# Interleaving the value projections with the chunk preparation, splitting the first inversion between GpSimd and VectorE, and starting the chunk loop one late-layer step later

## The reference

```python
q = _causal_conv_silu(x @ Wq.T, conv_q)     # also k, and v (128 wide a head)
q, k = _l2_norm(q), _l2_norm(k)
alpha = jnp.exp(-jnp.exp(A_log) * jax.nn.softplus(a_lin + dt_bias))
beta = 2.0 * jax.nn.sigmoid(x @ Wb.T)
...
S = a_t * (S - b_t * kkS) + jnp.einsum('bhd,bhv->bhdv', k_t, v_t)
o_t = jnp.einsum('bhdv,bhd->bhv', S, q_t)
```

## Time and profile before

| quantity | value |
|---|---|
| median of three runs | 9192.65 us |
| the profiled execution | 9168.5 us, span 9166.7 us |
| mean granted TensorE clock | 0.884 of full speed |
| TensorE matmul busy | 7076.2 us, 77% |
| VectorE busy | 4884.4 us, 53% |
| GpSimd busy | 2815.9 us, 31% |
| ScalarE busy | 2654.0 us, 29% |
| bytes moved by DMA | 225.76 MB, 25 GB/s |

### The profile page before, as it was taken

How to read it: one execution, slowest core, us unless ns; L and a number is a source line. 1 busy time by engine, 2 the same in 40 slices (tenths; PEclk the granted TensorE clock), 3 DMA queues, 4 the chain that set the end, 5 groups by cost and what they waited for, 6 DMA issues and landing times. The chain is left out here.

```text
span 9166.7 us, 157275 instructions
## 1 busy us (share of the span) xinstructions
PE 7076.2 (77%) x57416; PEld 5025.6 (55%) x57416; DVE 4884.4 (53%) x9955; ACT 2654.0 (29%) x5274; POOL 2815.9 (31%) x3681
## 2 busy tenths in 40 slices
PE   6787877777787787877878778777877878778786
PEld 3655646555465564645546465564655646456464
DVE  5555465454644546545464554546445464454643
ACT  2323232232422314223242332323223242232421
POOL 2414133141421414224142331424315142141421
PEclk9898988898898888988889889898888989889898
DMA  1100101001000100000000010010100100000000
GB/s 50 29 22 18 37 13 29 24 18 42 18 19 24 26 34 18 19 28 22 33 18 20 30 29 24 18 42 8 29 24 18 42 18 19 28 22 33 18 19 5
DMA packets 376004, 225.76 MB, mean 25 GB/s; under 512 B 336881, under 2 KB 353393, under 8 KB 366961
## 3 DMA queue, kind: packets, MB, share of 16 engines
q1 hardware_dynamic: 375152, 214.71, 7.8%
HBM read 155.95 MB, written 58.72 MB: 23 GB/s over the span
## 5 line engine op out<-in xcount | busy, mean ns | idle before, releaser
L763 DVE SCALAR_TENSOR_TENSOR SC<-SC,CW 128x512 f32<-128x512 f32 x1536 | 1280.9, 835 | 234.1 <-DVEq L761 142.4
L1445 PE MATMUL PS<-CST,SC 128*128 128x128 f32 x2776 | 508.6, 327 | 787.1 <-PEq L1728 282.3
L1445 PEld LDWEIGHTS PS<-CST,SC 128*128 128x128 f32 x2776 | 365.6, 165 | 974.4 <-issue 960.5
L954 POOL TENSOR_TENSOR RSTD<-VAR,NHALF 128x2 f32<-128x2 f32 x200 | 143.8, 719 | 2448.2 <-POOLq L953 2440.1
L1442 PE MATMUL PS<-S,KQ 64*64 64x128 f32 x8192 | 752.3, 304 | 0.0
L1070 POOL TENSOR_TENSOR WO<-WO 128x30 f32<-128x30 f32 (+14 forms) x960 | 635.6, 662 | 136.4
L1102 POOL TENSOR_TENSOR FR<-MS,NHALF 128x8 f32<-128x8 f32 x128 | 211.5, 1653 | 1345.5 <-POOLq L1101 941.7
L1067 POOL TENSOR_TENSOR WO<-WO 128x30 f32<-128x30 f32 (+14 forms) x960 | 581.6, 606 | 132.1 <-issue 6.9
L1442 PE MATMUL PS<-XT,WV 128*128 128x512 f32 x1024 | 515.2, 643 | 114.3 <-PEq L1747 76.5
L1442 PEld LDWEIGHTS PS<-S,KQ 64*64 64x64 f32 x8192 | 545.4, 152 | 73.9 <-issue 73.3
L1442 PE MATMUL PS<-SC,CST 128*128 128x512 f32 (+1 forms) x848 | 397.4, 607 | 227.1 <-PEq L1781 179.0
(11 more groups left out here) (157 smaller groups left out, 13195.4 us busy)
## 6 DMA issues: line engine op xcount, KB each, us to landing
WV<-in_wv SPq DMA_DIRECT2D x16, 2048.0 KB, 13.2
WO<-in_wo SPq DMA_DIRECT2D x16, 2048.0 KB, 8.9
WQK<-in_wq SPq DMA_DIRECT2D x16, 1024.0 KB, 5.9
WQK<-in_wk SPq DMA_DIRECT2D x16, 1024.0 KB, 7.9
cells_in<-SC SPq DMA_DIRECT2D x128, 128.0 KB, 2.7
WO<-cells_in SPq DMA_DIRECT2D x32, 512.0 KB, 3.3
cells_out<-WO SPq DMA_DIRECT2D x32, 512.0 KB, 2.6
cells_nat<-WO SPq DMA_DIRECT2D x32, 512.0 KB, 3.6
```

What stands on the lines that cost most here:

```text
L763: op = v.scalar_tensor_tensor(y, pre[:, j:j + G], CW[:, i * TAPS + j:i * TAPS + j + 1], y, ALU.mult, ALU.add)
L954: q.tensor_tensor(out=RSTD[:, 2 * k:2 * k + 2], in0=VAR[:, 2 * k:2 * k + 2], in1=NHALF[:, 0:2], op=ALU.pow).then_inc(rstd_ready, 1)
L1445: return nc.tensor.matmul(out_, in_, ident, is_transpose=True, start=True, stop=True)
```

## The change

Both series of tiles become one, `projections()` over 32 tiles, on TensorE, ScalarE and VectorE. The scalars are done behind tiles 18, 19 and 20 (`norms`, `by_chunk`, `decayed` on VectorE), and chunk c is prepared beside tile 21 + c (`PREP = QK_TILES + 5`): VectorE masks chunk c behind its tile (`masks`) and writes `PT_ALL` and `AT` of it in front of the next tile's taps (`grams`). PSUM is dealt out anew: value tiles have banks 0 to 2, the transposed values 3 and 4, and the preparation 5 to 7, one chunk at a time.

On GpSimd the inversion of the first half is cut in two. Steps 1 to 16 go, four at a time, behind the work for chunks 4 to 7; steps 17 to 30, the diagonal and the transposed copy go to VectorE, between the first late-layer steps of the recurrence. `FILL_FIRST` becomes 7, and the last chunk's counts lose a step. The core of the difference:

```diff
-FILL_FIRST = 6
-FILL = [(2, 2, 2)] * (CHUNKS - 2) + [(1, 1, 1)] * 3
+FILL_FIRST = 7
+FILL = [(2, 2, 2)] * 6 + [(1, 1, 1)] * 2 + [(1, 1, 0)]
+PREP = QK_TILES + 5
...
-            def projections(tiles):
-                for i in tiles:
+            def projections():
+                for i in range(CONV_TILES):
+                    c = i - PREP
+                    if 0 <= c - 1 < CHUNKS:
+                        grams(c - 1)
                     y, pre = Y[i % 5], PRE[i % 4]
...
+                    if i == QK_TILES + 2:
+                        norms()
+                    if i == QK_TILES + 3:
+                        by_chunk()
+                    if i == QK_TILES + 4:
+                        decayed()
+                    if 0 <= c < CHUNKS:
+                        masks(c)
+                conv_finish(CONV_TILES - 1)
...
-                fill(FILL_FIRST)
+                fill(1)
+                dve.wait_ge(sub_half, 1)
+                dve.sem_inc(sub_half, -1)
+                substitute(17, 21)
+                fill(1)
+                substitute(21, 26)
+                fill(1)
+                substitute(26, SUB - 1)
+                v.memset(M[:, 0:SUB * SUB:SUB + 1], 1.0)
+                dve.drain()
+                v.tensor_copy(v3(TMP, SUB), M.rearrange("p (j i) -> p i j", j=SUB))
+                dve.drain().then_inc(sub_first, 1)
+                fill(FILL_FIRST - 3)
                 keys(0)
...
+                for c in range(CHUNKS):
+                    pool.wait_ge(gam_ready, 1)
+                    pool.sem_inc(gam_ready, -1)
+                    if c + 1 < CHUNKS:
+                        sums(c + 1)
+                    pool.wait_ge(prep_used, 1)
+                    pool.sem_inc(prep_used, -1)
+                    scaled_query(c)
+                    if c + 1 < CHUNKS:
+                        scales(c + 1)
+                    if c == HALF:
+                        pool.wait_ge(m_loaded, 16)
+                        pool.sem_inc(m_loaded, -16)
+                    if c >= HALF:
+                        substitute(4 * (c - HALF) + 1, 4 * (c - HALF) + 5)
+                pool.drain().then_inc(sub_half, 1)
+                pool.drain().then_inc(qg_ready, 1)
...
+                    if i < CONV_TILES:
...
+                    if 0 <= c - 1 < CHUNKS:
+                        grams(c - 1)
+                    if i >= QK_TILES:
+                        after_conv(i - 3)
+                    if i == QK_TILES + 3:
+                        by_chunk()
+                    if i == QK_TILES + 4:
+                        sums()
+                    if 0 <= c < CHUNKS:
+                        decays(c)
```

More of the change, by code:

```diff
@@ new lines, in masks, with grams @@
+            def masks(c):
+                dve.wait_ge(dm_ready, 1)
+                dve.sem_inc(dm_ready, -1)
+                dve.wait_ge(mr_ready, 1)
+                dve.sem_inc(mr_ready, -1)
+                v.tensor_tensor(out=DM, in0=DM, in1=DB, op=ALU.mult)
+                dve.wait_ge(beta_ps, 1)
+                dve.sem_inc(beta_ps, -1)
+                dve.drain()
+                v.tensor_tensor(out=DB, in0=DM, in1=bank(7), op=ALU.mult)
+                dve.drain()
+            def grams(c):
+                for x in range(2):
+                    dve.wait_ge(kq_ps, 1)
+                    dve.sem_inc(kq_ps, -1)
+                    ps = bank(5 + x).rearrange("p (n k t) -> p n k t", n=4, k=2)
+                    at = c * G + x * 4 * C
+                    ns = slice(4 * x, 4 * x + 4)
+                    v.tensor_tensor(out=v3(PT_ALL[:, at:at + 4 * C], 4), in0=ps[:, :, 1, :], in1=v3(DM, PAIRS)[:, ns],
+                                    op=ALU.mult)
+                    i = v.tensor_tensor(out=v3(AT[:, at:at + 4 * C], 4), in0=ps[:, :, 0, :], in1=v3(DB, PAIRS)[:, ns],
+                                        op=ALU.mult)
+                    if x == 0:
+                        i.then_inc(gram_free, 1)
+                i.then_inc(at_ready, 1)
+                dve.drain().then_inc(gram_free, 1)
+                dve.drain().then_inc(prep_used, 1)
+                dve.drain().then_inc(dm_free, 1)
@@ L878, in projected, with substitute @@
                 v.tensor_tensor(out=xt, in0=xt, in1=bank(2)[:, 0:D], op=ALU.add).then_inc(wo_free, 1)
+            cells = M.rearrange("p (j i) -> p j i", j=SUB)
+            def substitute(first, last):
+                for j in range(first, last):
+                    w = SUB - 1 - j
+                    tmp = v3(TMP[:, 0:j * w], j)
+                    v.tensor_tensor(out=tmp, in0=each(cells[:, 0:j, j], j, w), in1=over(cells[:, j, j + 1:SUB], j, w),
+                                    op=ALU.mult)
+                    dve.drain()
+                    v.tensor_tensor(out=cells[:, 0:j, j + 1:SUB], in0=cells[:, 0:j, j + 1:SUB], in1=tmp, op=ALU.add)
+                    dve.drain()
             def recurrence(p):
@@ L937, in _ @@
                     decay_and_beta()
[L938 to L941, removed]
+                    projections()
                     recurrence(p)
@@ L1029, in tail @@
                 yield
[L1031 to L1058, removed]
             cells = M.rearrange("p (j i) -> p j i", j=SUB)
@@ L1391, in recurrence, with projections @@
                     pass
-            def projections(tiles):
-                for i in range(tiles[0], tiles[-1] + 5):
-                    if i <= tiles[-1]:
+            def projections():
+                for i in range(CONV_TILES + 5):
+                    if i < CONV_TILES:
                         act.wait_ge(proj_ps, 1)
@@ L1995, in _ @@
                 decay_inputs()
-                projections(range(QK_TILES))
-                scalars()
-                prepare()
-                projections(range(QK_TILES, CONV_TILES))
+                projections()
                 pe.wait_ge(b56_free, 2)
```

233 lines of the change are left out of this document (120 added, 113 removed).

## The result

The change makes the kernel slower, by 0.98%: 9281.83 us median of four runs (9262.92 to 9285.15) against 9192.18 for the kernel before, ratio 1.0098, 95% interval [1.0077, 1.0119]. I had forecast 9110, a gain; the time lies inside the range of 8885 to 9290, but on the wrong side of no change. The profiled execution took 9262.92 us.

The account below looks back on a forecast made before the run. VectorE bounded the value tiles; chunk preparation was a ring of waits with no engine full. -18.5 + 16.3 - 3.0 = -5.2 us a pass, x16 = -83: profiled 9168.5 becomes 9085, median 24 higher, so 9110 us; range 8885 to 9290.

Parts of the forecast that it names:

- The stream: Value tiles with chunk preparation, from tile 16 to the last finish: 114.4 us in place of 132.9, -18.5 us a pass.
- The bubble: Behind `norms`, ScalarE loads another table for its square root before copying tile 19: 4.00 us, bounds 1 and 8.
- a period: One chunk and its tile on VectorE: 6.7 us alone plus 3.0 from GpSimd's instructions, 9.7 us a chunk.
- The collision term: Each of GpSimd's four preparation instructions a chunk holds up VectorE by 0.75 us: 3.0 us a chunk, bounds 0 and 4.4.
- few collisions: Rival: GpSimd mostly falls beside VectorE instructions with a PSUM input; a chunk takes about 7.7 us, 8886 us in all; chance 0.18.
- the lock in full: Rival: GpSimd blocks VectorE for whole instructions and inversion steps delay masks; a chunk costs 11 us, 9375 us in all; chance 0.22.
- Where the collisions fall: In chunk preparation, GpSimd's products are released while VectorE runs taps, finish and L809, so nearly all collide.
- The start of the recurrence: Inverses now hang on VectorE; TensorE begins with them 31.5 us behind the last finish in place of 15.2: +16.3 us a pass.
- The clock: TensorE's clock may fall while it waits for the inverses; one of two alternatives for losing 5 us a pass.
- the third rival: The late-layer shift costs in the loop what it saves, or TensorE's clock falls: 9192 us, no change; chance 0.12.
- The shifted late layers: One late-layer step moves into TensorE's wait and the loop's `mix` waits less: -3 us a pass, bounds -7 and +3.
- The sum: Whole pass: -18.5 + 16.3 - 3.0 = -5.2 us, x16 = -83 us, giving 9110 us.

## Why the prediction was wrong

- **The stream, -18.5 us a pass:** right, a little small. From the first tap to the last finish it is 164.7 us in place of 186.4, -21.7. The bubble was 3.20 (I took 4.0), a period 9.5 to 9.7 in the mean (9.7). The collision term of 0.75 us for each of GpSimd's instructions measured 0.75 to 0.78 by leaving out the scaled query; the other three I didn't test singly. A period under 8 us, which few collisions needed, and one of 11, which the lock in full needed, are both excluded as a mean; the last two tap periods of the pass, 10.38 and 10.45, come near the second.
- **Where the collisions fall:** right in the main. I had named the taps, the finish and L829; the taps and finishes pay, while L829's median is 0.77 us, against 1.62 for L809. By the Trainium skill, "SBUF — State Buffer", section "SBUF: two separate sides", a VectorE instruction with two SBUF inputs and a GpSimd instruction that reads SBUF exclude each other for the whole instruction. A scaled query of 1.27 us or more that stands wholly beside taps would then cost its length, and leaving it out gave back 0.78. That is no clean test of the rule, since without the query GpSimd's next product starts beside the same taps.
- **The start of the recurrence, +16.3:** right, +16.6. VectorE's instructions, SP's way out and back and TensorE's first product came within 0.4 us. That steps 26 to 30 stood behind the wait for the first hidden tile was in my own working (12.3, then 15.5), and I priced it without seeing that it could be turned round; with nine steps in front, turning it round gave 0.6%.
- **The clock:** left out of the sum and named in the third rival. In pass two the stretch from the first small product to the state products grew by 2.6 us, at a clock of 0.50 in place of 0.72.
- **The shifted late layers, -3:** this is the step that failed. The shift adds 7.8 us a pass where I put -3, with +3 as the worse bound. Without it the change is worth -35 us, just my -2.2 us a pass. That this agrees so well is in part luck: the stream gained 3.2 us more than forecast and the clock took 2.6. I looked at one wait of the mix, 5.49 us in chunk 2, and held that one step of lead would shorten it. It did: that mix now starts at 932.22 behind a wait of 0.72. But the first mix, which waited for nothing in the trace of before and met its inputs with 0.3 us to spare, was moved past chunk 1's solve by the same edit. I had asked of the moved step what it waits for, and not of every later step which chunk product it now stands in front of. A look at where step 15 falls in both tables would have told it: group two of chunk 1 before, group one after.
- **The sum:** a pass went from 558.9 to 564.6, +5.7. Of that -21.7 + 16.6 + 2.6 are the terms above, which leaves 8.2 for the rest of the pass, near the 7.8 of the shift.
- **The rivals:** the third named the right places, the shift and the clock, but priced them at 5 us a pass above the forecast. The shift alone came 10.8 above it and the clock 2.6, against which stand only 3.2 more of the stream, so its 9192 was 90 us too low.

What stays open: why the new table costs 11 us a pass in the kernel before and 7.8 in the change, and what waits in chunk 5 when the shift is turned round.

## What to carry to other kernels

In an order written by hand, a step moved at one end shifts every later step against the work between them. Look at each place where a step crosses a product of the critical chain: a step ahead of its inputs holds up everything behind it on an in-order engine. A wait that a change makes is room: the table with nine steps in front made the kernel before 0.2% slower, and behind the new wait it was worth 1.7% against the old table. With the old table the change gave 0.4%, with nine in front 2.1%.

## What the runs showed of the hardware

A TensorE that waited 8.5 us ran the next 13.6 us wholly at a granted clock of 0.50, and 128 products of 32x32 then took 3.8 us of work in place of 2.2. Sixteen float32 matmuls of 128x512 take 13.9 us at a clock of 1.00, 0.87 us each, twice the upper end of what I had put. Leaving out GpSimd's scaled query, 1.27 us and more long, shortened the stream by 0.78 us a period, neither nothing nor its length. Four rows of the mix on VectorE took 3.06 us beside GpSimd's steps and 1.67 without them.
